# Cross-attention and mixture-of-experts layer: the last token group is split into its two parts before the first returned rows are read, and three groups' shared sums go through ScalarE into memory

## The reference

```
logits = x @ router_weight.T;  probs = softmax(logits);  topv, topi = top_k(probs, 4)
topv = topv / sum(topv)
out  = sum over the 4 chosen of 32 experts of topv * (silu(x w_gate) * (x w_up)) w_down
shared = silu(x @ sw_gate) * (x @ sw_up) @ sw_down           # one "shared expert" of width 512
out = out + sigmoid(x @ sgate_w) * shared
```

## Time and profile before

| what | value |
|---|---|
| median of 3 runs | 502.21 us (502.06 to 503.6) |
| profiled execution, its own time | 502.63 us |
| span of the profiled execution | 500.5 us |
| PE busy | 492.3 us (98%) |
| DVE busy | 363.7 us (73%) |
| ACT busy | 287.1 us (57%) |
| POOL busy | 272.1 us (54%) |
| granted TensorE clock | full (1.00) |

### The profile page before, as it was taken

How to read it: one execution, slowest core, us unless ns; L and a number is a source line. 1 busy time by engine, 2 the same in 40 slices (tenths; PEclk the granted TensorE clock), 3 DMA queues, 4 the chain that set the end, 5 groups by cost and what they waited for, 6 DMA issues and landing times.

```text
span 500.5 us, 13284 instructions
## 1 busy us (share of the span) xinstructions
PE 492.3 (98%) x3945; PEld 432.7 (86%) x3945; DVE 363.7 (73%) x1199; ACT 287.1 (57%) x719; POOL 272.1 (54%) x344
## 2 busy tenths in 40 slices
PE   7999999999999999999999999999999999999997
PEld 6999999999998888788888888888888888878886
DVE  5557888999886748834566777677767767379997
ACT  5777777877776635226477766677776662210110
POOL 2000477777777788881066767676676767500000
PEclk9999999999999999999999999999999999999999
DMA  6475577767745237934367666586766652399986
GB/s 212 136 224 184 172 255 222 220 222 214 219 165 179 101 110 181 250 132 108 91 186 229 202 197 195 174 238 182 217 197 194 183 188 101 96 402 377 327 361 208
DMA packets 65956, 100.77 MB, mean 201 GB/s; under 512 B 9856, under 2 KB 52864, under 8 KB 65792
## 3 DMA queue, kind: packets, MB, share of 16 engines
q1 hardware_dynamic: 48704, 60.30, 41.2%
q0 software_dynamic: 12672, 35.41, 19.5%
q10 hardware_dynamic: 4512, 4.23, 2.6%
HBM read 55.92 MB, written 43.97 MB: 200 GB/s over the span
## 4 chain that ended last, share of the span: by engine, by line
PE 90%; DVE 4%; DMA 2%; issue 1%; POOL 1%; ACT 1%; POOLq 0%; DVEq 0%; ACTq 0%; SPq 0%
PE bank L812 32%; PE bank L1108 14%; PE bank L1137 9%; PE bank L856 7%; PE bank L1104 5%; PE bank L1055 5%; PE bank L987 3%; PE bank L1018 3%; PE bank L1133 3%; PE bank L1004 3%; PE bank L1119 2%; PE bank L869 1%; PE bank L846 1%; POOL returned L515 1%; PE bank L972 1%
## 5 line engine op out<-in xcount | busy, mean ns | idle before, releaser
L484 POOL DMA_INDIRECT sent<-rows,slot x128 | 132.3, 1033 | 84.9 <-issue 83.6
L515 POOL DMA_INDIRECT returned<-arena,back x136 | 130.8, 962 | 77.1 <-DVE back L1638 35.6
L1108 PE MATMUL bank<-w_gu,arena 128*128 x416 | 79.7, 335 | 0.3 <-DVE resid L1278 0.3
L1108 PEld LDWEIGHTS bank<-w_gu,arena 128*128 128x128 f32 x416 | 66.3, 189 | 0.5 <-issue 0.5
L1606 DVE TENSOR_SCALAR arena<-bank,back_to 128x256 f32<-128x256 f32 x136 | 59.0, 475 | 3.0 <-issue 1.5
L542 ACT ACTIVATE act_t<-bank 128x512 f32<-128x512 f32 x24 | 14.4, 599 | 75.4 <-PE bank L812 75.4
L712 ACT COPY hnt<-w_gu 128x384 f32 x128 | 55.7, 511 | 0.0
L739 ACT ACTIVATE arena<-bank 128x192 f32<-128x192 f32 x68 | 22.4, 330 | 56.9 <-PE bank L1137 28.7
L1589 DVE TENSOR_TENSOR arena<-bank,arena 128x192 f32<-128x192 f32 x68 | 24.2, 356 | 41.6 <-ACT arena L739 40.2
L812 PE MATMUL bank<-w_hi_all,att_split 128*128 128x256 f32 x256 | 48.6, 292 | 0.0
L812 PE MATMUL bank<-hnt_rounded,ws_hi 128*128 128x512 f32 x160 | 48.4, 396 | 0.0
(11 more groups left out here) (216 smaller groups left out, 1057.3 us busy)
## 6 DMA issues: line engine op xcount, KB each, us to landing
arena<-returned SPq DMA_DIRECT2D x16, 1024.0 KB, 6.5
loaded<-sent SPq DMA_DIRECT2D x104, 134.0 KB
w_gu<-w_gate_up SPq DMA_DIRECT2D x32, 192.0 KB
sent<-rows SPq DMA_DIRECT2D x4, 1072.0 KB, 6.2
loaded<-sent SPq DMA_DIRECT2D x128, 33.5 KB
resid<-x SPq DMA_DIRECT2D x16, 256.0 KB, 3.7
att_plain<-ctx_t SPq DMA_DIRECT2D x16, 256.0 KB, 3.8
out<-resid ACTq DMA_DIRECT2D x7, 512.0 KB, 4.6
```

The source lines that it names most:

```text
L484: pool.indirect_dma_start(out=sent, out_offset=bass.IndirectOffsetOnAxis(ap=slot[:, 2 * b + j, k:k + 1], axis=0), in_=rows[:, u, j, :], in ...
L515: pool.indirect_dma_start(out=returned, out_offset=bass.IndirectOffsetOnAxis(ap=back[:, t:t + 1], axis=0), in_=down_e[u][:, s, :], in_offs ...
L1108: last = pe.matmul(view[:, s, :], rows_t[:, s, c, :], w_gu[:, c, bass.ds(e[s], 1), :] .rearrange("p e f -> p (e f)"), start=(c == 0), stop ...
```

## The change

Three things are edited.

One: the high part of group 7 gets a place of its own, `hn_hi_last`, in the memory of the expert weights `w_gu`, which nobody reads any more in the last stage. ScalarE makes it before the first silu of group 4, and VectorE makes the low part right behind the last copy of the experts' results, ahead of the first `shared_mul` of group 4.

Two: for groups 4, 5 and 6, `shared_add` is replaced by two steps. ScalarE's `scale_sums` multiplies the four tiles' down products by the gate and writes them to one of two places `scaled` in the memory of `w_gu`. VectorE's `scaled_add` adds all four tiles to `resid` with one instruction; it stands behind the first `shared_mul` of the next group, ahead of that group's folds. Group 7 keeps its four separate additions.

Three: the down product of a group no longer waits for VectorE's additions of the group before but for ScalarE's `scale_sums`.

```diff
+        (gu_rounded,) = under(("gu_rounded", DC * EXPERTS * 2 * F, F32R))
         w_gu = sb("w_gu", [P, DC, EXPERTS, 2 * F])
+        dead_gu = w_gu[:, :, :, :].rearrange("p c e f -> p (c e f)")
+        scaled = [dead_gu[:, 1024 + 1024 * n:2048 + 1024 * n].rearrange("p (t d) -> p t d", t=4) for n in range(2)]
+        hn_hi_last = gu_rounded[:, 0:DC * GT * P].rearrange("p (c t) -> p c t", c=DC)
...
-            return {0: 0, 1: 0, 2: FB, EARLY: FB * EARLY, EARLY + 2: 0, EARLY + 3: FB * (EARLY + 1)}.get(g, FB * g if g < EARLY else FB * (g - 1))
+            return {0: 0, 1: 0, 2: FB, EARLY: FB * EARLY, EARLY + 2: 0, EARLY + 3: 0}.get(g, FB * g if g < EARLY else FB * (g - 1))
...
+            def scale_sums(g):
+                wait(act, "shared_psum", sums_until(g) + 1)
+                wait(act, "shared_added", GT * (g - 1) if g > BEHIND + 1 else 0)
+                for t in range(GT):
+                    last = act.activation(scaled[g % 2][:, t, :],
+                                          sum_banks[t // 2][:, 256 * (t % 2):256 * (t % 2) + 256], ACT.Copy,
+                                          scale=shared_gate[:, GT * g + t:GT * g + t + 1])
+                last.then_inc(S["sums_scaled"], 1)
...
+            split_hn_hi(EARLY + 3)
             stored = 0
             for g in range(BEHIND, groups):
+                if g > BEHIND:
+                    scale_sums(g - 1)
                 for f in range(FB):
                     shared_silu(g, f)
-                    if g == BEHIND and f == FB - 1:
-                        split_hn_hi(EARLY + 3)
...
             def shared_down(g, behind={}):
-                wait(pe, "shared_added", GT * g)
+                wait(pe, "shared_added", GT * min(g, BEHIND))
+                wait(pe, "sums_scaled", g - BEHIND)
...
+            def scaled_add(g):
+                wait(dve, "sums_scaled", g - BEHIND + 1)
+                four = resid[:, GT * g:GT * g + GT, :]
+                dve.tensor_tensor(four, four, scaled[g % 2], ALU.add).then_inc(S["shared_added"], GT)
...
             expert_down_copy(pairs - 1)
+            split_hn_lo(EARLY + 3)
...
             for g in range(BEHIND, groups):
                 for f in range(FB):
                     shared_mul(g, f)
+                    if f == 0 and g > BEHIND:
+                        scaled_add(g - 1)
                     while weighed < weighed_by(g, f):
                         fold(weighed, g)
                         weighed += 1
                 wait(dve, "pick_step", weighed)
-                shared_add(g)
-                if g == BEHIND:
-                    split_hn_lo(EARLY + 3)
+                if g == groups - 1:
+                    shared_add(g)
```

More of the change, by code:

```diff
@@ L245, in build_xattn_moe @@
             "meant_ready", "meant_both_ready", "back_to_ready", "back_ready",
-            "sg_psum", "su_psum", "silu_ready", "shared_act", "shared_psum", "unit_psum", "shared_added",
+            "sg_psum", "su_psum", "silu_ready", "shared_act", "shared_psum", "unit_psum", "shared_added", "sums_scaled",
             "pick_step", "first_gates", "fold_step", "out_done")}
@@ L291, in hi_of @@
                 return logits_rounded[:, :].rearrange("p (c t) -> p c t", c=DC)
-            return group_of(hn_lo_all, EARLY - 1) if g in (EARLY, EARLY + 3) else hn_hi[:, :, :]
+            if g == EARLY + 3:
+                return hn_hi_last
+            return group_of(hn_lo_all, EARLY - 1) if g == EARLY else hn_hi[:, :, :]
         def hi_free(g):
-            return {0: 0, 1: 0, 2: FB, EARLY: FB * EARLY, EARLY + 2: 0, EARLY + 3: FB * (EARLY + 1)}.get(g, FB * g if g < EARLY else FB * (g - 1))
+            return {0: 0, 1: 0, 2: FB, EARLY: FB * EARLY, EARLY + 2: 0, EARLY + 3: 0}.get(g, FB * g if g < EARLY else FB * (g - 1))
         def unit_after(pair):
```

## The result

The changed kernel took 501.67 us (median of 20 runs, 501.0 to 503.65), the kernel before, run beside it, 502.51 us (20 runs). The medians differ by 0.84 us. The ratio on record, which is not the quotient of these two medians (that is 0.9983), is 0.9976 with a 95% interval of 0.9965 to 0.9987, a gain of 0.6 to 1.8 us. A second series on another chip gave 0.9981 (0.9967 to 0.9996). The forecast was 501.2 us and a gain of 1.05. The result lies inside the stated range of 500.4 to 502.4, and 0.07 us outside the narrower 500.9 to 501.6 that the prediction gave its own mechanism; the gain of under 0.3% that it forecast is what came.

The account below looks back on a forecast made before the run. TensorE (90% of the last-ending chain) and VectorE end almost together; TensorE gains 1.46 - 0.15 = 1.31, but VectorE bounds the end, so 502.21 - 1.05 = 501.2 us, range 500.4 to 502.4.

Parts of the forecast that it names:

- The place and the mechanism: VectorE between groups 4 and 5: low part and additions go, `scaled_add` comes, so `shared_mul` (5,1) starts 1.46 us earlier.
- One stop of TensorE: Before up product 3 of group 5, TensorE still idles once in the last stage, for 0.3 to 0.5 us.
- The held scatter: Ahead of group 4, the moved low part holds one GpSimd scatter, shifting later scatters and first load by 0.15 us.
- The rule on waits: Skill's claim that a semaphore between VectorE instructions costs nothing extra: `scaled_add` 1.14 us, where the rows gave 1.25.
- The sum: Adding the effects on TensorE and VectorE through group 7 to the last addition: 1.05 us gained.
- So VectorE bounds the end: At the end, VectorE's fourth final addition can start at 496.82, after TensorE's end at 496.52.
- TensorE's 1.31: From group 5 on, TensorE runs earlier by 1.46 less 0.15 for the scatter, 1.31 us.
- the exposed `scaled_add` of group 6: At group 7's start, this 1.25 us addition follows the waiting `shared_mul` (7,0); the next fold comes only 0.71 earlier.
- the final store is the same: After the last addition, the final store was taken as unchanged, so the addition's 1.05 us gain carries to the end.
- A: Rival, 20%: in group 5 stop and hold both vanish, TensorE gains 1.97 us, time 500.5.
- B: Rival, 22% with what lies between: the scatter ahead of group 4 is held 1.21 us, not 0.15; time 502.2.
- C: Rival, 6%: loads run late, one in group 7 takes 11.2 us, VectorE stands 2.2 us; time 503.4, slower.

Follow-up runs that it names:

- Split only: Against the kernel before, only group 7's high and low part moved to their new places, additions separate as before; 501.43 us against 502.55, ratio 0.9983.
- sums only: Against the kernel before, only the sums through ScalarE and `scaled_add`, group 7's split in its old place; 503.23 us against 502.55, ratio 1.0007.
- held longer: Changed kernel plus a useless 128x512 copy on VectorE ahead of group 7's low part; 502.45 us against 503.29 for the kernel before, ratio 0.9983.
- changed, again: The changed kernel, unedited, run again on another chip; 501.67 us against 502.55 for the kernel before, ratio 0.9981.
- add first: Changed kernel with group 6's `scaled_add` ahead of group 7's first multiplication; 501.42 us against 503.29 for the kernel before, ratio 0.9962.
- turns: Changed kernel with the third fold moved from behind multiplication (5,0) to group 5's end; 501.35 us against 503.29 for the kernel before, ratio 0.9963.
- all three: Changed kernel with a later low part, group 6's addition ahead of (7,0), third fold at group 5's end; 501.47 us against 503.29, ratio 0.9960.

## Why the prediction was right, point by point

**The place and the mechanism were right.** One stop of TensorE, 0.49 us where 0.3 to 0.5 stood; VectorE waits over 1 us at the start of group 7 (1.33); no wait before its last addition. "Split only" and "sums only" show what the steps implied: the gain is the 1.1 us low part taken from between groups 4 and 5 (0.82 in the stage), and the sums through ScalarE bring TensorE to group 7 0.37 earlier and cost more than that behind it, so that they make the stage 0.29 longer. In the working this stood as two separate remarks; it could have been said outright.

**The held scatter was right in kind and 0.07 short in size.** Forecast 0.15 for the scatter that the low part ends beside; measured 0.22 (1.18 against 0.96). The low part started 0.03 later against group 4's first product and the scatter 0.04 earlier than I had put them. Its moment, 0.13 us after the scatter's start, fits all cases: low part until 430.36, scatter ended 431.19, 0.83 later; in "held longer" 430.88 and 431.71, 0.83; in the earlier trace rows 0.83. In the other four profiles with the low part in this place ("changed, again", "split only", "add first", "turns") the scatter took 1.16, 1.13, 1.14 and 1.08 and ended 0.82 to 0.85 after the low part. Over these five executions with the same order around the low part the hold thus moves by 0.1 us.

The Trainium skill's SBUF — State Buffer, section "SBUF: two separate sides", on the shared port pair, was right in kind: a scatter waits for a VectorE instruction with two SBUF inputs. That each excludes the other for the whole instruction the rows do not bear out. The scatter at 428.75 was under way until 429.71 when the low part started at 429.14, and the low part took its usual 1.22, the scatter its usual 0.96.

**The rule on waits did not hold here.** By the Trainium skill's VectorE: DVE Perf Modes, section "The DRAIN you can't avoid", a semaphore between two VectorE instructions costs nothing extra, which the prediction had turned into 1.14 us for `scaled_add`. It kept the engine for 1.24 to 1.26 us (three cases).

**The sum was the step that failed, by half.** "So VectorE bounds the end" was right. But behind TensorE's 1.31 the sum took off only 0.26 for the exposed `scaled_add` of group 6 (1.31 - 1.05); it cost 0.67 (1.21 - 0.54). Stage times, where 1.05 us had been forecast and 0.54 measured:

| step | forecast gain | measured gain |
|---|---|---|
| first fold | -0.15 | -0.21 |
| TensorE at group 7 | 1.31 | 1.21 |
| fold behind (7,0) | 0.71 | 0.54 |
| first of the final additions | 0.71 | 0.55 |
| end of the last addition | 1.05 | 0.89 |
| issue of the last store | 1.05 | 0.65 |
| end of the span | 1.05 | 0.54 |

Of the 0.51 missing, 0.16 is the sum of small ones: 0.06 in the loads, 0.04 more until group 7, 0.05 in the wait of (7,0) (3.25 us behind group 7's first product in place of 3.20), 0.01 in `scaled_add`. The larger one is "the final store is the same". It was not. SP issues the four stores of the last group; the last one in the changed kernel:

```profile
498.93 0.45 SPq L440 DMA_DIRECT2D out<-resid  x1
```

and in the kernel before:

```profile
498.38 0.33 SPq L434 DMA_DIRECT2D out<-resid  x1
```

The last addition had ended at 498.66. Before, with a wait between the third and the fourth addition, SP issued 0.03 us after the last one; now the additions come every 0.40 us, an issue takes up to 0.45 in these rows, and SP is 0.27 behind. That is 0.24 lost. The last 0.11 lie between the last store's issue and the end of the span (2.25 against 2.14), and I can't name their cause. That all of it hangs on where the addition stands is shown by "add first", where the whole 0.67 is gone; how it splits into waits, queue and rest is read from the rows of one pair of executions.

**Outside the span 0.38 came that nobody had forecast**, and the two errors nearly cancel: 0.54 + 0.38 = 0.92 against 1.05, where the two series measured ratios worth 1.2 and 1.0 us and medians 0.84 and 0.88 apart. All kernels with `scale_sums` spend 1.73 to 1.75 us outside, the kernel before and split only 2.08 to 2.12. What happens there the trace doesn't show. The right total is thus partly luck.

**The rivals.** A fell: the stop stayed, and "turns" shows what its removal would have given (0.80). Its price was right: with stop and hold both gone, in "all three", TensorE reaches group 7 2.00 us earlier than before, where A had put 1.97. B fell: the hold was 0.22; "held longer" shows that 0.6 us of position make it 0.76, and the 1.21 of B was never met. C fell: no fold after the first waited for a load in any of the ten profiles, though the median load took 7.5 us in the changed kernel in place of 6.5. One small sum is off: a hold of 0.92 in place of 0.15 leaves 0.28 of the 1.05, which is 501.9 and not the 502.0 that the prediction wrote.

## What to carry to other kernels

An instruction whose inputs are ready should stand ahead of one that waits, not behind it: the same addition made the last stretch 0.67 us longer behind the multiplication and nothing longer ahead of it. When two engines end almost together, a gain on one is cut to the slack of the other and of the queue that issues the last stores. And an instruction moved into a quiet place of its own engine must be held against what the neighbouring engines do there: beside a back-to-back chain of scatters, 0.6 us of position made 0.6 us of time.

## What the runs showed of the hardware beyond that

- The low part, a VectorE subtraction of 128x1024 with two inputs in SBUF, delays a scatter of GpSimd as if the scatter could be held at one moment only, 0.13 us after its start, and the scatter ends 0.82 to 0.85 us after the low part (seven cases). Scatters that had been under way for 0.29 to 0.39 us when the low part began still took 0.96 (five cases); what happens between 0.13 and 0.29 us no case shows. Multiplications with one input in PSUM and the copy out of PSUM held none.
- Weighing 128x256 out of PSUM takes ScalarE 0.476 us each and 1.57 for four, close to the 1.6 taken.
- The first matmuls of an execution may run at about half their rate (2.04 and 2.00 us in place of 1.10 for four, until about 10 us) while the granted clock is given as 1.00. It cost 1.2 us, and four of ten profiled executions had it.
